# Attention times values with its probabilities loaded as four column quarters instead of two column halves

## The chip, the core and the metric

The kernel runs on one core of one Trainium2 chip. The metric is the device time of one execution in microseconds (us). A core has five engines with instruction streams of their own: TensorE (PE in the profile; PEld is its loading of weights), VectorE (DVE), ScalarE (ACT), GpSimd (POOL) and SyncE (SP), which issues the transfers here. They wait for each other by semaphores.

## What is computed

The input x holds four images of 128 channels and 112 x 112 pixels. Two residual blocks follow each other:

```
x = x + window_attention(group_norm(x))     # 8x8 windows, 8 heads of 16 channels, layer norm in front
x = x + linear_attention_block(group_norm(x))   # k^T v context, 3x3 depthwise taps, projection, MLP of 1024
```

Only the first block matters here. In it an image is cut into 14 x 14 windows of 64 tokens. Per window and head:

```
scores = einsum('nhqd,nhkd->nhqk', q * scale, k)
attn = softmax(scores)
o = einsum('nhqk,nhkd->nhqd', attn, v)
```

The last of these lines is the product that is changed. All inputs and outputs are FP32.

## The kernel before, in words

The program has three stages: A/B, the window attention over all four images (until about 1165 us); C, a pass over the images that gathers the linear attention's context (until about 1510 us); D, the linear attention's output, the depthwise taps and the MLP. The change is in the first alone.

There the work goes by *groups* G. An image has 14 strips of 8 rows, a strip has 14 windows, that is 7 window pairs, and a strip is two groups: `gg = 0` with four pairs and `gg = 1` with three (GROUP_PAIRS). group_loop (L301) unrolls strip 0, loops over strips 1 to 11 (Fori) and unrolls strips 12 and 13 of each image. All engines walk through the same groups, each in an order written out by hand in its own `step` function, software-pipelined over several groups. For group G the step of TensorE (L1348) is:

1. score_rows(G) (L1289, bf16), waiting for the exponentials of G-1; DVE takes the row maxima from it (maxima, L940).
2. out_transpose(G-2) (L1328); a wait for the values of G (v_ready).
3. attend(G-1, h=1) (L1320), window pairs 2 and 3 of the group before.
4. ln_transpose(G+2) (L1244), out_project(G-2) (L1334).
5. attend(G-1, h=0) (L1320), window pairs 0 and 1 of the group before.
6. transpose_maxima(G) (L1295), waiting for DVE's maxima.
7. project_q(G+1) and project_k(G+1) (split_mm, L1255 to L1257). project_q waits for oh_ready[1] of G-1, because its output goes to bank 7, which attend(G-1, h=1) wrote and DVE's normalise (L953, L957) reads.
8. score_cols(G) (L1304, L1308): scores with keys in the partitions, of which ACT makes the exponentials (exps, L663) into `prob`.
9. project_v(G+1) (L1272), ln_back(G+2) (L1250).

DVE's step (L989) is maxima(G), normalise(G-1, h=1), ln_stats(G+2) (L911), mt_evac(G) (L946), ln_moments(G+2) (L919), normalise(G-1, h=0), in the second group of a strip strip_stats (L963, reading ximg), ln_norm(G+2) (L926, waiting for POOL's L508), v_evac(G+1) (L933, waiting for project_v), and in the first group of a strip, in all images but the last, next_stats (L963, reading xs): the group-norm statistics of a strip of the next image. Strip 0 has them three times, strips 12 and 13 not at all. At strip 12 the group norms of the next image (and of the one before) are put together across DVE, TensorE and POOL.

attend has, per window pair t and head quad j, the keys of two heads in the 128 partitions of `prob` and 64 queries of one window in its columns; the moving operand `vx` has 34 columns (two heads of 16 channels and a column of ones that gives the softmax denominator). The outputs of the pair's two windows lie in partitions 0 to 63 and 64 to 127 of bank 6 or 7. An FP32 matmul call shows in the trace as two weight loads and two matmuls.

Of the kernel before, what the change touches and what calls it, by code (L numbers as in the profile page):

```python
# [41 lines left out]
QUADS = 4  # L42
VCOLS = 2 * (HD + 1)
# [29 lines left out]
def build(nc, x_d, vec_d, fc1b_d, dw_d, wm_d, cm_d, w1_d, w2_d, sel_d, out_d):  # L73
    with ExitStack() as ctx:
        def sb(name, shape, dt=F32, stack=ctx):
            return stack.enter_context(nc.sbuf_tensor(name, shape, dt))
# [16 lines left out]
        w2 = sb("w2", [P, NF, P])  # L93
# [49 lines left out]
        vx = sb("vx", [P, 2, 8, QUADS, VCOLS], F32, stack_b)  # L143
# [14 lines left out]
        prob = sb("prob", [P, QUADS, 8, 64], F32, stack_b)  # L158
# [27 lines left out]
        bank = [ctx.enter_context(nc.psum_tensor(f"bank{n}", [P, 512], F32)) for n in range(8)]  # L186
# [1034 lines left out]
        def _(pe):  # L1221
            mm = nc.tensor.matmul
# [90 lines left out]
            def attend(G, gg, h):  # L1313


                for t in range(2 * h, min(2 * h + 2, GROUP_PAIRS[gg])):
                    for j in range(QUADS):
                        for w2 in range(2):
                            c = (t % 2) * QUADS * VCOLS + j * VCOLS
                            m = mm(bank[6 + h][64 * w2:64 * w2 + 64, c:c + VCOLS],  # L1320
                                   prob[:, j, 2 * t + w2, :], vx[:, gg, 2 * t + w2, j, :], start=True, stop=True)
                m.then_inc(pv_mm, 1)

            def out_transpose(G, gg):
# [23 lines left out]
            def step(G, i, s, gg, near):  # L1348
# [6 lines left out]
                if near(-1):  # L1355
                    attend(G - 1, ng, 1)
# [5 lines left out]
                if near(-1):  # L1362
                    attend(G - 1, ng, 0)
# [19 lines left out]
            def epilogue():  # L1383
                pe.wait_ge(ob_ready, NG - 2)
                out_transpose(NG - 2, 0)
                pe.wait_ge(prob_ready, NG)
                pe.wait_ge(v_ready, NG)
                attend(NG - 1, 1, 1)
                out_project(NG - 2, 0)
                attend(NG - 1, 1, 0)  # L1390
                pe.wait_ge(ob_ready, NG - 1)
                out_transpose(NG - 1, 1)
                out_project(NG - 1, 1)
# [196 lines left out]
```

## Time and profile before

| | us |
|---|---|
| median of three runs (2786.65 to 2791.28) | 2789.6 |
| the profiled execution, its own time | 2789.54 |
| its span | 2787.7 |
| TensorE matmuls busy, share of the span | 94% |
| TensorE weight loads | 78% |
| DVE | 81% |
| ACT | 77% |
| POOL | 49% |

Matmuls are pipelined, so a busy TensorE is not one at its peak, and the time between the starts of two instructions tells more than the length of one. In merged rows of the timeline the first figure is the start of the first instruction, the second the time from there to the end of the last, and the last is how many there are.

### The profile page before, as it was taken

What the parts mean: (1) busy time and instruction counts of PE and PEld (TensorE: products, weight loads), DVE (VectorE), ACT (ScalarE), POOL (GpSimd) and SP (SyncE); (2) the same over time, 40 slices, a digit from 0 to 9 for tenths busy, and PEclk for the clock granted to TensorE, in tenths of its full rate; (3) what the DMA queues carried; (4) which work ended last, traced back from release to release, by engine and by line L of the source; (5) the groups of instructions that cost most, each with busy time, mean ns of one, the idle gap of its engine ahead of it and who ended that gap; (6) DMA issues with size and microseconds to landing.
All of it is one profiled execution on the core that took longest, in us unless ns stands there. A gap on an engine that the chain in (4) does not pass through costs nothing.

```text
span 2787.7 us, 76479 instructions
## 1 busy us (share of the span) xinstructions
PE 2615.0 (94%) x28138; PEld 2176.2 (78%) x28138; DVE 2267.2 (81%) x5003; ACT 2134.8 (77%) x3921; POOL 1369.2 (49%) x1322
## 2 busy tenths in 40 slices
PE   2999899999999999899979999999999999999999
PEld 2777777777777777699968888888888888888887
DVE  4888788878888888577778888888888888888885
ACT  1677677767776777455569999999999999999997
POOL 1445445545555555345525555555555555554554
PEclk9999999999999999899989999999999999999999
DMA  4222122212221111133301111111011111100000
GB/s 137 66 67 79 54 81 71 73 55 87 66 72 42 53 53 40 50 124 114 116 24 41 40 37 40 40 41 39 31 40 40 40 40 38 39 27 20 20 19 22
DMA packets 55758, 151.60 MB, mean 54 GB/s; under 512 B 6608, under 2 KB 20944, under 8 KB 55632
## 3 DMA queue, kind: packets, MB, share of 16 engines
q1 hardware_dynamic: 55632, 149.93, 16.7%
q8 instruction: 78, 1.28, 0.2%
q14 instruction: 48, 0.39, 0.0%
HBM read 98.52 MB, written 51.38 MB: 54 GB/s over the span
## 4 chain that ended last, share of the span: by engine, by line
PE 86%; ACT 6%; DVE 3%; issue 3%; DMA 1%; POOL 1%; SPq 0%; DVEq 0%; POOLq 0%; ACTq 0%
PE bank L1255 14%; PE bank L1257 14%; PE bank L1256 13%; PE bank L1487 12%; PE bank L1320 7%; PE bank L1308 7%; ACT prob L663 5%; PE bank L1408 5%; PE bank L1416 3%; PE bank L1334 3%; PE bank L1328 2%; PE bank L1244 2%; PE bank L1289 2%; PE bank L1304 1%; DMA ximg<-x_in 1%
## 5 line engine op out<-in xcount | busy, mean ns | idle before, releaser
L598 POOL TENSOR_TENSOR hl<-hf,hh 128x448 fp32r<-128x448 f32 x448 | 517.5, 1155 | 637.9 <-ACT hh L791 637.9
L1139 DVE SCALAR_TENSOR_TENSOR bank<-oring,dw,bank 128x448 f32<-128x448 f32 x896 | 614.8, 686 | 20.1
L1487 PE MATMUL bank<-hw,w 128*128 128x448 f32 x896 | 391.2, 538 | 0.0
L1255 PE MATMUL bank<-t1h,w_hi 128*128 128x448 f32 x896 | 364.9, 407 | 6.0 <-DVE t1l L1156 6.0
L788 ACT ACTIVATE hf<-bank,fc1b 128x448 f32<-128x448 f32 x448 | 282.5, 631 | 111.8 <-PE bank L1257 111.8
L1257 PE MATMUL bank<-t1l,w_hi 128*128 128x448 f32 x896 | 325.7, 364 | 0.0
L1256 PE MATMUL bank<-t1h,w_lo 128*128 128x448 f32 x896 | 323.0, 360 | 0.0
L1320 PEld LDWEIGHTS bank<-vx,prob 128*64 128x64 f32 x6272 | 205.8, 140 | 98.8 <-issue 83.5
L791 ACT ACTIVATE hh<-hf 128x448 fp32r<-128x448 f32 x448 | 259.2, 578 | 14.1
L782 ACT ACTIVATE hw<-bank,fc1b 128x448 f32<-128x448 f32 x448 | 265.9, 618 | 0.4 <-PE bank L1257 0.4
L663 ACT ACTIVATE prob<-bank 128x512 f32<-128x512 f32 x448 | 207.4, 549 | 75.9 <-PE bank L1308 75.9
L514 POOL TENSOR_TENSOR xn_lo<-xn,xn_hi 128x512 fp32r<-128x512 f32 x112 | 128.1, 1144 | 278.3 <-ACT xn_hi L640 278.3
L940 DVE TENSOR_REDUCE mx<-bank 128x8 bf16<-128x512 f32 x448 | 248.5, 617 | 10.2 <-PE bank L1289 7.2
L933 DVE COPY vx<-bank 64x256 f32<-64x256 f32 x448 | 174.2, 389 | 85.3 <-PE bank L1272 80.7
L1320 PE MATMUL bank<-vx,prob 128*64 128x34 f32 x6272 | 231.2, 228 | 2.1 <-ACT prob L663 0.7
L542 POOL TENSOR_TENSOR ximg<-ximg,ob 128x512 f32 (+1 forms) x112 | 127.8, 1141 | 210.0 <-ACT ob L676 210.0
L1487 PEld LDWEIGHTS bank<-hw,w 128*128 128x128 f32 x896 | 168.9, 189 | 49.4 <-issue 41.8
L1255 PE MATMUL bank<-hh,w_hi 128*128 128x448 f32 x448 | 202.0, 451 | 0.7 <-POOL hl L598 0.7
L1308 PE MATMUL bank<-qs,kx 32*128 32x64 f32 x6272 | 202.3, 277 | 0.0
L1255 PEld LDWEIGHTS bank<-t1h,w_hi 128*128 128x128 f32 x896 | 168.8, 188 | 35.6 <-issue 20.8
L584 POOL TENSOR_TENSOR xw<-wb,ximg 128x448 f32<-128x448 f32 x112 | 172.4, 1540 | 46.1 <-ACT wb L773 33.6
L676 ACT ACTIVATE ob<-bank,vec 128x512 f32<-128x512 f32 x112 | 71.2, 636 | 160.9 <-PE bank L1334 160.9
(156 smaller groups left out, 6865.7 us busy)
## 6 DMA issues: line engine op xcount, KB each, us to landing
ximg<-x SPq DMA_DIRECT2D x112, 448.0 KB, 3.4
ximg<-x_in SPq DMA_DIRECT2D x56, 448.0 KB, 3.4
x<-ximg SPq DMA_DIRECT2D x56, 448.0 KB, 2.5
y_out<-yb SPq DMA_DIRECT2D x112, 224.0 KB, 1.9
xs<-x_in SPq DMA_DIRECT2D x42, 448.0 KB, 3.4
wm<-wm_in SPq DMA_DIRECT2D x1, 512.0 KB, 3.7
w1f<-w_in SPq DMA_DIRECT2D x1, 512.0 KB, 5.4
w<-w_in SPq DMA_DIRECT2D x1, 512.0 KB, 7.1
```

What stands on the lines that cost most here:

```text
L598: g.tensor_tensor(hl[:, k, :], hf[:, k % 2, :], hh[:, k, :].bitcast(F32), ALU.subtract).then_inc(hl_ready, 1)
L663: m = a.activation(prob[:, j, 0:n // 64].rearrange("p w q -> p (w q)"), bank[j][:, 0:n], ACT.Exp)
L782: a.activation(hw[:, WHOLE_J.index(j), :], bank[j % FC1_BANKS][:, 0:BLOCK], ACT.Gelu, bias=fc1b[:, j:j + 1]).then_inc(hf_ready, 1)
L788: a.activation(hf[:, k % 2, :], bank[j % FC1_BANKS][:, 0:BLOCK], ACT.Gelu, bias=fc1b[:, j:j + 1]).then_inc(hf_ready, 1)
L791: a.activation(hh[:, k, :], hf[:, k % 2, :], ACT.Copy).then_inc(hh_ready, 1)
L1139: m = d.scalar_tensor_tensor(acc, src, dw[:, k:k + 1], acc, ALU.mult, ALU.add)
L1255: mm(out, w[0], x[0], start=start, stop=False)
L1256: mm(out, w[1], x[0], start=False, stop=False)
L1257: return mm(out, w[0], x[1], start=False, stop=stop)
L1308: m = mm(bank[j][:, 64 * w:64 * w + 64], kx[quad_rows(j), gg, w, :, :].rearrange("p s k -> p (s k)"), qs[quad_rows(j), gg, w, :], start=Fa ...
L1320: m = mm(bank[6 + h][64 * w2:64 * w2 + 64, c:c + VCOLS], prob[:, j, 2 * t + w2, :], vx[:, gg, 2 * t + w2, j, :], start=True, stop=True)
L1487: m = mm(out, w2[:, j, :], hw[:, WHOLE_J.index(j), :], start=first, stop=last)
```

## The change

Each call of 64 queries becomes two of 32. Four consecutive calls now write partitions 0, 32, 64 and 96 of the bank: windows 0 and 1 of the pair, each in two parts. `vx` is read once per part, so each window's values stream twice. Banks, columns, sums and the semaphore at the end are as before.

```
--- before.py
+++ after.py
@@ -1315,10 +1315,11 @@
                 for t in range(2 * h, min(2 * h + 2, GROUP_PAIRS[gg])):
                     for j in range(QUADS):
-                        for w2 in range(2):
-                            c = (t % 2) * QUADS * VCOLS + j * VCOLS
-                            m = mm(bank[6 + h][64 * w2:64 * w2 + 64, c:c + VCOLS],
-                                   prob[:, j, 2 * t + w2, :], vx[:, gg, 2 * t + w2, j, :], start=True, stop=True)
+                        for q in range(4):
+                            c, w = (t % 2) * QUADS * VCOLS + j * VCOLS, 2 * t + q // 2
+                            m = mm(bank[6 + h][32 * q:32 * q + 32, c:c + VCOLS],
+                                   prob[:, j, w, 32 * (q % 2):32 * (q % 2) + 32], vx[:, gg, w, j, :],
+                                   start=True, stop=True)
                 m.then_inc(pv_mm, 1)
```

## Rows read from the trace of the kernel before

**Rows 1.** The page: busy time of the engines, and the weight loads of L1320.

```profile
PE 2615.0 (94%) x28138; PEld 2176.2 (78%) x28138; DVE 2267.2 (81%) x5003; ACT 2134.8 (77%) x3921; POOL 1369.2 (49%) x1322
...
L1320 PEld LDWEIGHTS bank<-vx,prob 128*64 128x64 f32 x6272 | 205.8, 140 | 98.8 <-issue 83.5
```

**Rows 2.** Busy time by stretch: ten strips of image 1, twelve of the last.

```profile
core 0: us, PE busy (x) PEld busy (x) DVE busy (x) ACT busy (x) POOL busy (x), PEclk, DMA share, GB/s
378.40:569.10 190.70, 176.43 (x3610) 142.25 (x3611) 165.71 (x511) 137.73 (x241) 97.79 (x120) 1.00 0.23 72
888.80:1117.70 228.90, 211.97 (x4332) 170.76 (x4333) 185.68 (x589) 165.35 (x289) 117.27 (x144) 1.00 0.14 49
```

**Rows 3.** The same stretches, DVE's statistics (L963) alone.

```profile
378.40:569.10 190.70, 23.08 (x40) 1.00 0.23 72
888.80:1117.70 228.90, 13.82 (x24) 1.00 0.14 49
```

**Rows 4.** The chain of waits through the ten strips of image 1, by line.

```profile
by line: PE bank L1320 20.1%; PE bank L1308 16.9%; ACT prob L663 14.9%; PE bank L1334 7.9%; issue 6.0%; PE bank L1328 5.6%; PE bank L1244 5.6%; PE bank L1255 4.9%; PE bank L1257 4.3%; PE bank L1256 4.3%; PE bank L1289 4.2%; PE bank L1304 3.
```

**Rows 5.** Groups by shape, 100 to 1000 us: busy us, mean ns | idle before.

```profile
L1320 PEld LDWEIGHTS bank<-vx,prob 128*64 128x64 f32 x5152 | 166.3, 138 | 79.1 <-issue 67.9 <-DVE vx L933 11.2
L1308 PEld LDWEIGHTS bank<-qs,kx 32*128 32x128 f32 x5112 | 155.3, 192 | 0.0
...
L1334 PE MATMUL bank<-ot,wm 128*128 128x512 f32 x92 | 47.1, 594 | 0.0
```

**Rows 6.** Timeline of one strip of image 1, weight loads.

```profile
426.38 0.24 PEld L1289 LDWEIGHTS bank<-k,q 32*64 32x64 bf16 x24 [1.16 <-issue]
...
427.19 1.01 PEld L1320 LDWEIGHTS bank<-vx,prob 128*64 128x64 f32 x32 [0.17 <-issue]
...
430.44 0.20 PEld L1255 LDWEIGHTS bank<-xn_hi,pw_hi 128*128 128x128 f32 x1
...
436.65 0.55 PEld L1320 LDWEIGHTS bank<-vx,prob 128*64 128x64 f32 x16 [0.27 <-DVE vx L933]
...
439.75 0.20 PEld L1255 LDWEIGHTS bank<-xn_hi,pw_hi 128*128 128x128 f32 x1
...
441.20 1.87 PEld L1308 LDWEIGHTS bank<-qs,kx 32*128 32x128 f32 x64
443.14 0.74 PEld L1272 LDWEIGHTS bank<-wm,xn 128*128 128x128 f32 x6
```

**Rows 7.** The same strip, matmuls.

```profile
426.42 0.37 PE L1289 MATMUL bank<-k,q 32*64 32x128 bf16 x24 [0.95 <-ACT prob L663]
...
437.74 1.02 PE L1334 MATMUL bank<-ot,wm 128*128 128x512 f32 x2
```

**Rows 8.** The same strip, DVE.

```profile
429.86 0.42 DVE L957 TENSOR_TENSOR oh<-bank,rden 128x256 f32<-128x256 f32 x1
...
434.87 1.73 DVE L933 COPY vx<-bank 64x256 f32<-64x256 f32 x4 [0.88 <-PE bank L1272]
...
439.26 0.29 DVE L957 TENSOR_TENSOR oh<-bank,rden 128x128 f32<-128x128 f32 x1
```

**Rows 9.** Timeline of one strip of the last image, weight loads of project_q.

```profile
998.10 0.20 PEld L1255 LDWEIGHTS bank<-xn_hi,pw_hi 128*128 128x128 f32 x1
...
1007.41 0.20 PEld L1255 LDWEIGHTS bank<-xn_hi,pw_hi 128*128 128x128 f32 x1
```

**Rows 10.** The same strip of the last image, DVE.

```profile
996.69 0.42 DVE L957 TENSOR_TENSOR oh<-bank,rden 128x256 f32<-128x256 f32 x1
...
1006.92 0.29 DVE L957 TENSOR_TENSOR oh<-bank,rden 128x128 f32<-128x128 f32 x1
```

**Rows 11.** DMA queues, 293 to 377 us (image change), then 378 to 569 us (loop).

```profile
q1 hardware_dynamic: 1584, 5.05, 19.5%
q8 instruction: 12, 0.20, 1.0%
...
q1 hardware_dynamic: 4359, 13.85, 22.7%
```

## The prediction, before the changed kernel was run

> **What bounds the kernel now.** I read the page first. TensorE has the largest share, 2615.0 us of a span of 2787.7, and VectorE (DVE) follows with 2267.2 [rows 1]. The line that changes is L1320, the product of probabilities and values: 6272 weight loads, each with one matmul, 140 ns for a load [rows 1]. All of them lie in the window attention, so only that stage matters. Next I cut out two steady stretches of it and asked for the busy time of each engine. Ten strips of image 1 take 190.7 us and twelve of the last image 228.9: 19.07 us a strip in both. TensorE is busy 93% of each, DVE 87% in the one and 81% in the other [rows 2]. The difference is the statistics of the next image (L963 reading xs), which the last image has not: 40 instructions in ten strips against 24 in twelve, so four a strip against two, 2 x 23.08 / 40 = 1.15 us of DVE work less [rows 3]. That a strip lasts 19.07 us with and without this work says that DVE doesn't set the pace. The chain of waits through image 1 says what does: L1320 is its largest part, 20.1%, then the scores L1308, then the exponentials on ScalarE (ACT) [rows 4]. So L1320 is on the path. The question is how far the path can shorten before DVE, busy 87%, is next.
>
> **What the change does to L1320.** An FP32 call is two loads and two matmuls. Before, one head quad and pair is two calls (four loads, four matmuls), each on one half of the array's columns. After, it is four calls on four quarters: twice as many instructions, each load half as wide (32 columns), each matmul still streaming 34.
>
> What a load costs is seen by comparing three lines. Six full loads of L1272 (128 columns, one after the other) take 0.74 us, and one load of that width lasts 0.19: (0.74 - 0.19) / 5 = 110 ns apart. L1308 loads 128 columns too, but into four separate row strips in turn: 64 loads in 1.87 us, so (1.87 - 0.19) / 15 = 112 ns per four. Four loads into different parts take the time of one. L1320 loads 64 columns into two halves in turn: 32 loads in 1.01 us, (1.01 - 0.138) / 15 = 58 ns per two [rows 5, 6]. Half the width, half the time, two side by side. A load therefore takes about 0.83 to 0.9 ns per column in its own part, and single loads agree: 192 ns for 128 columns, 138 for 64 [rows 5]. A matmul: two of L1334 (512 columns) take 1.02 us, one 594 ns, so 426 ns for 512 columns or 0.83 per column [rows 5, 7]; 34 columns are 28 ns, hidden today beside a load of 53 to 58.
>
> No row has four column quarters at work. A quarter's load should be 32 x 0.83 = 27 ns, its matmul 28. Lower bound of a step in which all four quarters do one load and one matmul: 28 ns. Upper bound, if load and matmul of one part take turns (58 = 30 + 28 today): 15 + 28 + 2 = 45. I take 33, the matmul's 28 plus the 5 by which today's step exceeds 64 x 0.83 = 53: the row of L1308 is nearest, where load and matmul plainly overlap (107 + 53 would be more than 112).
>
> A step of two halves (58) thus becomes a step of four quarters (33) and their number stays: 25 ns saved each. A strip has 112 loads, so 56 steps. In the first half of the strip shown (from L1289 x24) two stretches of 16 steps save 0.80 us, in the other 8 + 16 steps save 0.60: 1.40 us of TensorE per strip, 78 us in 56 strips. Nothing else is added: no wait, no buffer, no transfer, and no queue of SP or POOL is touched.
>
> **How much of it reaches the end.** After the second L1320 stretch TensorE transposes the maxima and starts project_q, L1255, which must wait until DVE has finished L957, the normalised output of the first stretch (oh_ready[1]). Today TensorE comes later than that and the wait costs nothing. In image 1 L957 ends at 429.86 + 0.42 = 430.28 and L1255's load starts at 430.44; in the other half 439.55 and 439.75 [rows 6, 8]. A semaphore takes 0.05 us: L933 ends at 436.60 and the L1320 waiting for it loads at 436.65 [rows 6, 8]. So the slack is 0.11 and 0.15 us, and beyond it TensorE stands waiting, with both projections, the scores and project_v queued behind. DVE's next copy of V waits for project_v, its statistics and maxima follow without a pause, and L957 comes after them: a ring in which the rest of DVE's work is closed. A strip with statistics can shorten by 0.11 + 0.15 = 0.26 us, whatever L1320 saves beyond.
>
> In the last image the 1.15 us of statistics are missing, so the maxima come earlier: in the first half L957 ends at 997.11 and L1255 loads at 998.10, a slack of 0.94 after the semaphore, and the whole 0.80 arrives. The other half again has 1007.41 - 1007.21 - 0.05 = 0.15 [rows 9, 10]. Sum 0.95 us a strip. ACT's exponentials, which delay L1289 by up to 0.95 us [rows 7], start when the scores end and only shift along.
>
> Sum, by the code's 14 strips per image: strips 1 to 11 of three images, 33 x 0.26 = 8.6; the last image but its strip 12, 13 x 0.95, and the three other strips 13, which have no statistics, 3 x 0.95: 15.2; strip 0 of three images and strip 12 of four, where images change over and group norms are computed, between 0 and 0.95 each, half taken: 3.3. Together 27 us. The profiled execution took 2789.54 us, 1.8 around its span, and is as good as the median of 2789.6; 2789.5 - 27 gives **2762 us**, 1.0% faster. At 45 ns a step the last image's strips gain 0.42 + 0.15 and the sum is about 20 (2770); at 28 ns it is some 29.
>
> The clock stood at 1.00 in both stretches [rows 2] although TensorE idled 0.95 us at a time there; the new idle before L1255 is shorter, so I cost it at nothing. At an image change a half-speed stretch could come or go; that is in the range.
>
> **Rivals.**
> 1. *Two parts at a time.* If only two of the four quarters can be fed at once, because all four read the same 128 partitions, four take two steps, 66 ns against 58: 8 x 56 = 0.45 us a strip on a path that is TensorE's already, 25 us more in 56 strips: **2815**. It decides as soon as four take over 58. For it: L1308's four parts read 32 partitions each, so no row shows four readers of one partition. Against: L1289 runs row strips and column halves together, 24 loads in 0.24 us [rows 6]. 8%.
> 2. *A floor per FP32 instruction.* L1308 and L1320 both issue a load every 27 to 28 ns (1.68 / 63, 0.872 / 31) [rows 6]. If this is a floor and no coincidence, four quarters take 112 ns, 54 more a step, 3.0 us a strip: 169 more, **2959**. Against it stands L1289 in bf16, 6 ns apart. 4%. The Trainium skill states such a floor (TensorE: Matmul & The Clock Gate, Back-to-back issue gap): starts never come closer than about 25 ns, however few the columns. By it four would take 100 ns and the estimate is 130 us more. L1289's row disagrees with it where parts alternate.
> 3. *The loop's code.* Around an image change 12 fetches bring 0.20 MB for four strips of straight code, 50 KB a strip; in the ten looped strips there is no fetch at all [rows 11]. Ten strips hold 3611 loads and 3610 matmuls [rows 2], 722 a strip; 224 more make the body 65 KB. If that no longer stays, each of 40 jumps back waits for one or two fetches of 1.1 us (1.0% of 16 engines over 84 us, by 12): 44 to 88 more, less 27: about **2830**. 3%. The Trainium skill (Runtime: NRT & Kernel Launch, Instruction fetch mechanics) gives TensorE 128 KiB, which would hold it.
> 4. *The slack is nowhere.* The last image is held by some other wait too, or the quarters save little: every strip gains about 0.2, 10 us, **2779**. 10%, half of it counted as faster.
> 5. *DVE gives way,* its order leaving more room than I see, and most of the 78 arrives: **2715**. 3%.
>
> **How the numbers follow.** My forecast has 72%. A measurement of this kernel tells 0.2%, 5.6 us, from no change. Faster by more: 72 + 3 + 5 = 80%; the same: the other 5%; slower: 8 + 4 + 3 = 15%. The range reaches up to 2788, where rival 4 ends, and down to 2748 (statistics strips at twice 0.26 for 9 us more, change-over strips in full for 3), and holds the forecast and rival 4, 82%.
>
> **What would show it.** L1320 with 12544 loads and matmuls; 64 loads in about 0.6 us rather than 32 in 1.01; strips of 18.8 us in image 1 and 18.1 in the last; L1255 now waiting for DVE's L957 some 0.5 us in each half strip; DVE about 88% busy. Wrong would be: 64 loads in over 1.0 us (rivals 1, 2), instruction fetches inside the loops (3), or strips of equal length in images 1 and 3 (4, 5).

## The result, and the profile after

The changed kernel takes 2767.2 us (median of five runs, 2762.1 to 2774.0) against 2789.6 before. That is 22 us faster, where 27 were forecast; by the means of five runs each it is 20 us (ratio 0.9927, 95% interval 0.9900 to 0.9954). The profiled execution is the slowest of the five, 2774.0 us; steady strips are compared in it below, and the total by the medians.

Part of the 22 us goes along with TensorE's clock. In both profiles strips 2 to 11 of every image have the full 2.4 GHz. Stretches at half of it lie in strips 0, 1 and 12, at the changes of stage and once within stage C. (By the trace stage D begins near 1411 us, and not at 1510.) The mean granted clock differs from run to run, and the time with it:

| granted clock, mean of a run (1 is 2.4 GHz) | before, us | changed, us |
|---|---|---|
| 0.980 | 2791.7 (mean of 12, 2789.9 to 2792.7) | 2774.0 |
| 0.984 | 2783.1 (mean of 2) | 2767.2 |
| 0.985 | 2781.5 | 2765.5 (mean of 3, 2762.1 to 2768.2) |

The column of before takes in the runs made beside the experiments. At the same granted clock the change is worth 16 to 18 us. The five runs of the change have 0.984 in the mean, 29 of the kernel before 0.981, and that goes with the rest of the 22, some 5 us. Whether the change itself brings more of the full clock is open.

The page of the changed kernel: busy time, the chain by engine (first that of the kernel before, then that of the changed one), and the loads of L1320.

```profile
PE 2566.4 (93%) x34410; PEld 2115.2 (76%) x34410; DVE 2266.5 (82%) x5003; ACT 2133.4 (77%) x3921; POOL 1368.6 (49%) x1322
...
PE 86%; ACT 6%; DVE 3%; issue 3%; DMA 1%; POOL 1%; SPq 0%; DVEq 0%; POOLq 0%; ACTq 0%
PE 77%; DVE 15%; issue 4%; ACT 2%; DMA 1%; POOL 1%; DVEq 0%; SPq 0%; POOLq 0%; ACTq 0%
...
L1320 PEld LDWEIGHTS bank<-vx,prob 128*32 128x32 f32 x12544 | 131.2, 110 | 103.1 <-issue 86.2
```

There are twice as many loads as in [rows 1], and one is 110 ns long instead of 140. TensorE is busy 49 us less, DVE as long as before. Here is the timeline of TensorE in a strip of image 1, weight loads first. (In this kernel lines behind L1320 carry numbers one higher.)

```profile
428.53 0.66 PEld L1320 LDWEIGHTS bank<-vx,prob 128*32 128x32 f32 x64 [0.17 <-issue]
...
431.73 0.19 PEld L1255 LDWEIGHTS bank<-xn_hi,pw_hi 128*128 128x128 f32 x1 [0.58 <-issue]
...
440.95 0.19 PEld L1255 LDWEIGHTS bank<-xn_hi,pw_hi 128*128 128x128 f32 x1 [0.38 <-issue]
```

Its matmuls, to the start of the next strip:

```profile
427.75 0.37 PE L1289 MATMUL bank<-k,q 32*64 32x128 bf16 x24 [0.86 <-ACT prob L663]
...
431.76 0.48 PE L1255 MATMUL bank<-xn_hi,pw_hi 128*128 128x512 f32 x1 [0.48 <-DVE oh L957]
...
440.98 0.41 PE L1255 MATMUL bank<-xn_hi,pw_hi 128*128 128x384 f32 x1 [0.28 <-DVE oh L957]
...
446.68 0.37 PE L1289 MATMUL bank<-k,q 32*64 32x128 bf16 x24 [0.87 <-ACT prob L663]
```

And DVE's L957, for which project_q waits:

```profile
431.19 0.43 DVE L957 TENSOR_TENSOR oh<-bank,rden 128x256 f32<-128x256 f32 x1
...
440.54 0.29 DVE L957 TENSOR_TENSOR oh<-bank,rden 128x128 f32<-128x128 f32 x1
```

A stretch of 64 loads takes 0.66 us where 32 took 1.01 [rows 6]: (0.66 - 0.11) / 63 = 8.7 ns a load, 35 per four quarters. TensorE then stands before project_q, 0.48 us in one half strip and 0.28 in the other, waiting for DVE: the wait that cost nothing before [rows 6, 8]. The strip lasts 446.68 - 427.75 = 18.93 us, against 19.07. The chain through ten strips of image 1 has changed hands: DVE's maxima head it, and L1320, 20.1% in [rows 4], is no longer among the larger parts.

```profile
by line: DVE mx L940 23.7%; PE bank L1308 16.2%; PE bank L1272 10.6%; DVE vx L933 9.9%; issue 9.0%; PE bank L1255 6.8%; DVE gst L963 5.5%; PE bank L1256 4.3%; PE bank L1257 4.1%; DVE oh L957 3.9%; PE bank L1304 3.1%; DVE rden L953 1.6%; DVE
```

In the last image, which has no statistics to gather, the same rows show only one of the two waits. Weight loads:

```profile
986.62 0.24 PEld L1289 LDWEIGHTS bank<-k,q 32*64 32x64 bf16 x24 [1.07 <-issue]
...
989.95 0.20 PEld L1255 LDWEIGHTS bank<-xn_hi,pw_hi 128*128 128x128 f32 x1
...
999.18 0.19 PEld L1255 LDWEIGHTS bank<-xn_hi,pw_hi 128*128 128x128 f32 x1 [0.39 <-issue]
...
1004.88 0.24 PEld L1289 LDWEIGHTS bank<-k,q 32*64 32x64 bf16 x24 [1.07 <-issue]
```

DVE:

```profile
989.26 0.43 DVE L957 TENSOR_TENSOR oh<-bank,rden 128x256 f32<-128x256 f32 x1
...
998.77 0.29 DVE L957 TENSOR_TENSOR oh<-bank,rden 128x128 f32<-128x128 f32 x1
```

In the first half L957 is done at 989.69 and TensorE comes at 989.95, so it doesn't wait. In the second it waits until 0.12 us behind L957's end. The strip is 18.26 us long, 0.81 shorter than before. In the looped strips no code is fetched, as before [rows 11]: a window of the queues from 380 to 565 us holds data alone.

```profile
q1 hardware_dynamic: 4190, 13.32, 22.4%
```

### The profile page after: what moved, and what is told of

Its sections match the earlier page's. It is cut to its first block, busy times and chain, and to the rows that moved or that the text cites. A ratio compares the mean times of both kernels' runs of the same rounds, so it can differ in the third digit from the quotient of the medians.

```text
span 2772.2 us, 89023 instructions
## 1 busy us (share of the span) xinstructions
PE 2566.4 (93%) x34410; PEld 2115.2 (76%) x34410; DVE 2266.5 (82%) x5003; ACT 2133.4 (77%) x3921; POOL 1368.6 (49%) x1322
## 4 chain that ended last, share of the span: by engine, by line
PE 77%; DVE 15%; issue 4%; ACT 2%; DMA 1%; POOL 1%; DVEq 0%; SPq 0%; POOLq 0%; ACTq 0%
PE bank L1255 15%; PE bank L1257 14%; PE bank L1256 14%; PE bank L1488 12%; DVE mx L940 7%; PE bank L1308 7%; PE bank L1409 5%; PE bank L1272 3%; DVE vx L933 3%; PE bank L1417 3%; DVE gst L963 1%; PE bank L1320 1%; ACT prob L663 1%; PE bank L1304 1%; DVE oh L957 1%
## 5 line engine op out<-in xcount | busy, mean ns | idle before, releaser
L1139 DVE SCALAR_TENSOR_TENSOR bank<-oring,dw,bank 128x448 f32<-128x448 f32 x896 | 614.8, 686 | 20.1
L933 DVE COPY vx<-bank 64x256 f32<-64x256 f32 x448 | 174.0, 388 | 84.3 <-PE bank L1272 79.6
L1320 PEld LDWEIGHTS bank<-vx,prob 128*32 128x32 f32 x12544 | 131.2, 110 | 103.1 <-issue 86.2
L1308 PEld LDWEIGHTS bank<-qs,kx 32*128 32x128 f32 x6272 | 195.3, 196 | 0.0
L1256 PEld LDWEIGHTS bank<-t1h,w_lo 128*128 128x128 f32 x896 | 168.7, 188 | 31.6 <-issue 20.8
```

The costliest lines, as they stand in the source:

```text
L933: m = d.tensor_copy(dst, src)
L1139: m = d.scalar_tensor_tensor(acc, src, dw[:, k:k + 1], acc, ALU.mult, ALU.add)
L1256: mm(out, w[1], x[0], start=False, stop=False)
L1308: m = mm(bank[j][:, 64 * w:64 * w + 64], kx[quad_rows(j), gg, w, :, :].rearrange("p s k -> p (s k)"), qs[quad_rows(j), gg, w, :], start=Fa ...
```

## The experiments

The theory: in images 0 to 2 a ring of DVE work, closed through project_q's wait for L957, sets the strip and swallows most of what L1320 saves. Its rivals: the quarters or their code are slower than thought, so that TensorE itself saves little. Beside it two questions came up: what sets the quarters' pace of 8.7 ns, and why strips around an image change gained so little in the profile. The kernel before, run beside each batch, had medians of 2790.8 us for the first four, 2781.5 (one run) for the fifth and sixth, and 2790.3 for the last two.

### Statistics left out, with quarters

The statistics of the next image are gathered over 8 elements instead of 448, so that part of the computation is left out.

```
-                bn_halves(lambda h: gst1[:, bass.ds(n * 2 + h, 1), :].rearrange("p a c -> p (a c)"), xs)\
-                    .then_inc(xs_done, 1)
+                for h in range(2):
+                    m = d.bn_stats(gst1[:, bass.ds(n * 2 + h, 1), :].rearrange("p a c -> p (a c)"),
+                                   xs[:, h * BLOCK:h * BLOCK + 8])
+                m.then_inc(xs_done, 1)
```

> The changed kernel with the next image's group-norm statistics cut from 448 to 8 elements per instruction (that part of the computation is left out; the instructions, waits and signals stay). Theory: in images 0 to 2 a ring of DVE work closed through the wait of project_q for L957 sets the strip, so taking 1.1 us of DVE work out of it brings the steady strips from 18.94 down to the last image's 18.27 us; some 33 strips by 0.67, 22 us less than the change's 2767, about 2745. Rival: the strips of images 0 to 2 are longer for a cause on TensorE (the quarters' own pace, code fetched in the loop), and stay at 18.94; about 2767.

Measured: 2743.0 us, ratio 0.9821 (0.9805 to 0.9837). The scores that open two consecutive strips of image 1 (the line number has moved), and the cut statistics on DVE:

```profile
431.55 0.37 PE L1291 MATMUL bank<-k,q 32*64 32x128 bf16 x24 [0.87 <-ACT prob L663]
...
449.82 0.37 PE L1291 MATMUL bank<-k,q 32*64 32x128 bf16 x24 [0.87 <-ACT prob L663]
```

```profile
431.66 0.24 DVE L971 BATCH_NORM_STATS2 gst<-xs 128x8 f32 x2
```

With 0.24 us of statistics instead of 1.15 the strip of image 1 is 18.27 us long, the last image's to the hundredth. Work on DVE alone was taken away, and TensorE's strip became shorter: the ring holds. The rival falls.

### Statistics left out, with halves

The same cut in the kernel before.

> The kernel before with the same cut of the statistics (left out in the same way). Theory: TensorE sets the strip there, DVE has 1.15 us to spare, so the steady strips stay at 19.07 and the time at 2787 to 2790. Rival: DVE's work already shared the path before, and the strips fall below 19.0 and the time by 10 us or more.

Measured: 2781.0 us, ratio 0.9961 (0.9948 to 0.9974). The scores again:

```profile
427.77 0.37 PE L1291 MATMUL bank<-k,q 32*64 32x128 bf16 x24 [0.96 <-ACT prob L663]
...
446.85 0.37 PE L1291 MATMUL bank<-k,q 32*64 32x128 bf16 x24 [0.96 <-ACT prob L663]
```

The steady strip stays at 19.08 us, as the theory says: before the change, DVE's work was beside the path. The total is 6 us lower than expected all the same. Strip 1 of images 0 to 2 came down from 20.17 to 19.24 us. Here is that of image 1, first before, then in this run:

```profile
358.21 0.43 PE L1289 MATMUL bank<-k,q 32*64 32x128 bf16 x32 [0.19 <-ACT prob L663]
378.38 0.43 PE L1289 MATMUL bank<-k,q 32*64 32x128 bf16 x32 [0.44 <-ACT prob L663]
...
360.50 0.43 PE L1291 MATMUL bank<-k,q 32*64 32x128 bf16 x32 [0.44 <-ACT prob L663]
379.74 0.43 PE L1291 MATMUL bank<-k,q 32*64 32x128 bf16 x32 [0.44 <-ACT prob L663]
```

So there DVE did bind before the change, which the forecast had not seen; probably strip 0, with its three sets of statistics, hands the excess on. The three strips make 2.8 us. At the same granted clock, 0.982, this version takes 2785.7 us and the kernel before 2788.7 (mean of six), 3 us more, so what the medians show beyond that goes along with the clock.

### project_k ahead of project_q, with quarters

```
+                    cast_k(G + 1, ng)
                     cast_q(G + 1, ng)
-                    cast_k(G + 1, ng)
...
+                    k_evac(G + 1, ng)
                     q_evac(G + 1, ng)
-                    k_evac(G + 1, ng)
...
+                    if near(-2):
+                        pe.wait_ge(ob_ready, G - 1)
+                    project_k(G + 1, ng)
                     if near(-1):
                         pe.wait_ge(oh_ready[1], G)
                     project_q(G + 1, ng)
-                    if near(-2):
-                        pe.wait_ge(ob_ready, G - 1)
-                    project_k(G + 1, ng)
```

> The changed kernel with project_k ahead of project_q, and the conversions of both swapped on ACT and POOL. project_k doesn't wait for L957, so its 0.6 to 0.8 us pass while DVE finishes. Theory: the ring opens by that much, TensorE sets the pace again, the steady strips of all images fall to 18.0 to 18.3 us and the time to about 2745. Rival: q's conversion, now last on ACT, delays the exponentials or project_v by what the wait gave, and the strips stay at 18.9 or above; 2767 or more.

Measured: 2736.8 us, ratio 0.9796 (0.9783 to 0.9810). One strip of image 1, matmuls:

```profile
430.25 0.37 PE L1289 MATMUL bank<-k,q 32*64 32x128 bf16 x24 [0.60 <-ACT prob L663]
...
433.68 0.47 PE L1255 MATMUL bank<-xn_hi,pw_hi 128*128 128x512 f32 x1
...
434.46 0.40 PE L1255 MATMUL bank<-xn_hi,pw_hi 128*128 128x512 f32 x1
...
448.35 0.37 PE L1289 MATMUL bank<-k,q 32*64 32x128 bf16 x24 [0.60 <-ACT prob L663]
```

DVE:

```profile
433.69 0.42 DVE L957 TENSOR_TENSOR oh<-bank,rden 128x256 f32<-128x256 f32 x1
```

project_k starts at 433.68, when L957 has only begun; project_q follows at 434.46, when L957 (until 434.11) is long done, and neither row shows a wait. The strip is 18.10 us, in image 1 as in the last. The chain is TensorE's and ACT's again:

```profile
by line: PE bank L1308 17.7%; ACT prob L663 15.4%; PE bank L1320 13.8%; PE bank L1335 8.3%; PE bank L1255 6.6%; issue 6.2%; PE bank L1244 5.6%; PE bank L1329 5.6%; PE bank L1256 4.6%; PE bank L1257 4.6%; PE bank L1289 4.2%; PE bank L1304 3.
```

This version is 54 us faster than the kernel before and 30 faster than the change alone.

### The same order, with halves

The swap alone, in the kernel before.

> The kernel before with the same swap of order and nothing else. Theory: there the wait for L957 costs nothing (slack 0.05 to 0.1 us), so the swap alone leaves the strips at 19.07 and the time within 5 us of 2789. Rival: the order is worth something by itself, and the time falls to 2775 or less, in which case a gain of the swap with quarters isn't proof of the ring.

Measured: 2784.3 us, ratio 0.9971 (0.9959 to 0.9983). The steady strips stay at 19.08 us:

```profile
427.32 0.37 PE L1289 MATMUL bank<-k,q 32*64 32x128 bf16 x24 [0.95 <-ACT prob L663]
...
446.40 0.37 PE L1289 MATMUL bank<-k,q 32*64 32x128 bf16 x24 [0.96 <-ACT prob L663]
```

The order by itself is worth some 6 us by the medians, outside the steady strips. At the same granted clock it is 2 us or less (at 0.983 two runs have 2784.4 us in the mean, two of the kernel before 2786.6). Quarters alone give 22, the order alone 6, both together 54 by the medians; at the same granted clock 16 to 18, at most 2, and 49 (at 0.983 three runs of both together have 2737.2). The new order gains only where the quarters have made the wait bind, and the quarters' gain arrives only once the wait is out of the way.

### Matmuls of 17 columns

```
-                        for q in range(4):
+                        for n, q in enumerate([0, 1, 2, 3] * 2):
                             c, w = (t % 2) * QUADS * VCOLS + j * VCOLS, 2 * t + q // 2
-                            m = mm(bank[6 + h][32 * q:32 * q + 32, c:c + VCOLS],
-                                   prob[:, j, w, 32 * (q % 2):32 * (q % 2) + 32], vx[:, gg, w, j, :],
-                                   start=True, stop=True)
+                            s = n // 4
+                            m = mm(bank[6 + h][32 * q:32 * q + 32, c + 17 * s:c + 17 * s + 17],
+                                   prob[:, j, w, 32 * (q % 2):32 * (q % 2) + 32],
+                                   vx[:, gg, w, j, 17 * s:17 * s + 17], start=True, stop=True)
```

> The changed kernel with each matmul of 34 columns cut into two of 17, each with a load of its own: twice as many loads and matmuls, half the columns in each. Measured step of the change: 34 to 37 ns for four quarters, against 33 forecast. If the matmul's streaming sets it (28 ns of 34 columns plus an edge), a step of 17 columns falls to about 20 ns and 128 loads take 0.7 us, as 64 do now. If the loading of 32 columns (27 ns) or the rate at which TensorE is given instructions sets it, loads stay 8.6 ns apart and 128 take 1.1 to 1.2 us, and the strips lengthen by about 1 us.

Measured: one run of 2869.5 us. The loads of one stretch:

```profile
490.85 1.17 PEld L1321 LDWEIGHTS bank<-vx,prob 128*32 128x32 f32 x128 [0.55 <-issue]
```

(1.17 - 0.11) / 127 = 8.3 ns a load with half the columns, so the matmul's streaming doesn't set the step. The steady strips are 19.59 us in all images: 0.65 more than with 34 columns where there are statistics, 1.32 more in the last image, which waits for DVE in one half strip only and so has less waiting to absorb it.

### The bf16 scores three times over

```
-                for w in range(2 * GROUP_PAIRS[gg]):
+                for w in [*range(2 * GROUP_PAIRS[gg])] * 3:
```

> The changed kernel with the bf16 scores L1289 computed three times over into the same place: 96 and 72 loads in a run in place of 32 and 24. In the change's trace the loads of a stretch of L1320 come in fours for the first half of the 64 and then in pairs at 8.5 ns a load. If that is the pace at which instructions arrive once those prepared during the work before are used up, the 96 loads begin at 6.5 to 7 ns apart and go on at 8.5, some 0.75 us in all. If the array's parts set the pace in either line, they stay at 6.5 to 7 ns to the end, 0.65 us.

Measured: one run of 2802.6 us. The loads of 72 and of 96:

```profile
485.86 0.71 PEld L1289 LDWEIGHTS bank<-k,q 32*64 32x64 bf16 x72 [0.87 <-issue]
...
495.00 0.91 PEld L1289 LDWEIGHTS bank<-k,q 32*64 32x64 bf16 x96 [0.65 <-issue]
```

In the change's kernel the 32 of one score_rows take 0.30 us, 6.5 ns apart:

```profile
436.85 0.30 PEld L1289 LDWEIGHTS bank<-k,q 32*64 32x64 bf16 x32 [0.65 <-issue]
```

The 64 behind them add 0.61 us here, 9.5 ns each; starts read one by one show the first 32 in bursts, one gap of 0.1 us, and then an even 8.3 ns to the end. With 17 columns the starts behind the first 32 are 8.3 ns apart as well. bf16 scores and FP32 products have neither operands, widths nor parts in common, and run at one pace once 32 loads with their 32 matmuls have gone. The likeliest cause is the pace at which TensorE is handed instructions, about 8.3 ns for a load and a matmul; no run changes that pace alone, so it is not shown. Within the first 32 the quarters have a pace of their own: over the first sixteen loads four take 32 ns with 34 columns and 30 with 17. The Trainium skill gives TensorE a queue of 64 instructions (TensorE: Matmul & The Clock Gate, Architectural detail, on queue depths); the trace agrees, for 32 pairs are 64.

### Quarters in the loop only

The trace of the change has five places in unrolled strips where TensorE pauses inside a run of L1320 with no wait, over 0.4 us from one start of a matmul to the next, 3.8 us in all; the trace before has none. One of them, by the weight loads:

```profile
315.32 0.64 PEld L1320 LDWEIGHTS bank<-vx,prob 128*32 128x32 f32 x63 [0.76 <-issue]
317.55 0.11 PEld L1320 LDWEIGHTS bank<-vx,prob 128*32 128x32 f32 x1 [1.59 <-issue]
```

A window of the queues around it, 314 to 318 us, has one fetch of code:

```profile
q8 instruction: 1, 0.02, 1.5%
```

That made a theory: unrolled strips suffer from the longer code. The edit gives attend a number of parts, 2 where the strip is unrolled and 4 in the loop (against the kernel before; the operands' indices follow):

```
-                        for w2 in range(2):
+                        for q in range(parts):
+                            n = P // parts
...
+                parts = 2 if isinstance(s, int) else 4
```

> Quarters in the looped strips 1 to 11 only, halves in the unrolled strips 0, 12 and 13, where the change's trace shows TensorE standing still in the middle of L1320 for 0.6 to 1.6 us with no wait, each time resuming 1.3 to 1.5 us after a code fetch has landed. Theory: the doubled instructions outrun the fetching of code that is met for the first time; with halves there the pauses inside L1320 are gone, the strips around an image change are some 1 us shorter each and the time is 3 to 8 us below the change's 2767. Rival: those strips are set by the group norms and the clock; nothing changes there but the gain of quarters that is lost, and the time is 2767 to 2770. Looped strips stay at 18.94 and 18.27 by both.

Measured: 2779.4 us, ratio 0.9964 (0.9952 to 0.9976). The looped strips are 18.94 and 18.27 us as they should be, but the total is 12 us worse by the medians than with quarters everywhere, more than the rival said. About half of that goes along with the clock: at 0.980 this version takes 2780.2 us (mean of three) and the change 2774.0, and the eight runs here have 0.980 in the mean against 0.984. The theory falls as an account of those strips: quarters gain there too, some 6 us at the same clock, about half a microsecond in each of the 12. In the last image strip 0 takes 19.07 us here and 18.27 with quarters.

> The same restriction to the looped strips, with project_k ahead of project_q. Theory: looped strips at 18.10 us as measured with k first, strips around an image change without pauses inside L1320, 3 to 8 us below the 2737 of k first alone. Rival: 2737 or up to 5 us more, as the unrolled strips lose what quarters save.

Measured: 2742.6 us, ratio 0.9837 (0.9821 to 0.9852), 6 us above the version with quarters everywhere. The intervals of the two don't touch. The pauses themselves are real: with quarters in the loop only they are found in strip 1 of images 0 and 3, the first pass through the loop's code (with q first 0.4 and 0.75 us at 83 and 93 us, 0.5 and 0.7 at 907 and 916; with k first 1.0 at 89 and at 884). They lie where the quarters' code is met for the first time, though not in all such places, and come to 2 to 4 us in all.

## Why the prediction was right, and where its sizes were off

**L1320 is on the path.** Right. Its share of the chain went from 20.1% to under what the chain's row lists.

**Four quarters run side by side.** Right: rivals 1 and 2 asked for 66 and 112 ns per four, and 35 were measured against 33 forecast. The reason I gave was not right. I took the matmul's 28 ns plus an edge; the run with 17 columns shows that streaming hardly matters (32 and 30 ns per four within the first 32 loads), and the scores done three times that behind the first 32 one pace holds for all, 4 x 8.3 = 33. That it lies so near the forecast is chance. The floor of 25 ns in the Trainium skill (TensorE: Matmul & The Clock Gate, Back-to-back issue gap), cited with rival 2, doesn't hold for matmuls in alternating parts: here they start 8.3 ns apart.

**The ring through project_q's wait.** Right, and shown from two sides: less DVE work shortens the strip to 18.27 us, and an order that doesn't need L957 so soon to 18.10. Its size was off, in one term: the reaction. I took 0.05 us from L933 to the waiting L1320. project_q's load comes 0.11 and 0.12 us behind L957's end (431.62 to 431.73, 440.83 to 440.95). Of the gaps of 0.16 and 0.20 in the rows before, that leaves 0.05 + 0.08 = 0.13 instead of 0.26, and the strip indeed lost 0.135. Strips 2 to 11 of three images then give 4.1 us. Strip 1, which DVE bound already before, went only from 20.17 to 20.11 us in images 0 and 2; the 33 strips together give 4.2 us, not 8.6.

**The last image.** Forecast 0.95 a strip, measured 0.81. With 35 ns the first half saves 32 x 23 ns = 0.74, the other 0.20 - 0.12 = 0.08. Sixteen such strips would give 13.0, not 15.2. Strips 0 to 11 of the last image did gain 0.8 each; the strips 13 of images 0 to 2 took 57.65 us in the profile against 57.22 before, with two of the pauses in the first of them.

**The changes of image.** I took 3.3 us for strips 0 and 12 by halving; with the two terms above the sum is 20.5. The medians say 22.4, but at the same granted clock it is 16 to 18; in the sum I had put the clock at nothing, and its stretches at image changes only into the range. So 22 lies that near 27 in part by luck: some 5 us of it go along with a higher granted clock. The two profiles, with 0.981 and 0.980, differ by 15.5 us, and 12.3 of these lie in strips 2 to 11 of the four images. Which other strips hold the rest is open: one profile differs from the next by up to 4 us in strip 12, with the stretches in which the clock is granted at half. (The range's lower end comes to 2750 by its own terms, not 2748.)

**Loop code (rival 3).** It didn't happen in the loop. A small relative of it did, in straight code: the five pauses of 3.8 us.

## What to carry to other kernels

Before pricing a saving on the busiest engine, look for the waits that cost it nothing today and ask when the other engine would be ready: here gaps of 0.16 and 0.20 us decided the gain of 33 strips, not the 1.4 us saved. A wait that becomes binding can often be moved behind work that doesn't need it, and then the two edits are worth more together (49 us at the same granted clock) than each alone (16 to 18, and at most 2). And take the time from a release to the waiting instruction from a row of that same instruction where there is one; 0.06 us per wait halved the gain of those strips. Where versions differ by a few microseconds, compare them at the same granted clock, or by strips that have all of it.

## What the runs showed of the hardware that was not expected

- In these stretches of small matmuls in alternating parts, TensorE starts a pair of load and matmul every 8.3 ns after the first 32, in FP32 and in bf16 alike; the first 32 pairs come 6.2 ns apart in bf16 and 7.5 to 7.8 in FP32. Splitting the product further than that bought nothing: 128 loads of 17-column matmuls took 1.17 us where 64 with 34 columns took 0.66.
- The load of project_q reacts 0.11 to 0.12 us after its release, that of L1320 0.05, in every strip from 378 to 566 us. No run here tells why.
- Code met for the first time can stop TensorE in the middle of a run of small matmuls, 0.4 to 1.7 us at a time, in the change's trace 1.2 to 1.5 us behind the landing of a fetch of code each; the kernel before shows no such pause inside L1320.
- The time of one kernel follows the granted clock of the run: the kernel before took 2798.7 us at 0.977 and 2781.5 at 0.985, with no stretch at half clock in its strips 2 to 11.
